# A hybrid layer's kernel: the butterfly folding woven into the first batch's mixer, its low stages multiplied together, and the last division moved to VectorE

## The reference

```python
xl = tanh((x + delta * xp_mu) @ xp_W1.T)          # delta = shifted - x
mur, muw, muk, muv, mug = per-token mixes from xl (rank 32 each)
r, k, v = (x + delta * mu_) @ W_.T                # w and g through rank 64 and tanh
o = rwkv6_scan(r, k, v, -exp(w), bonus)
x = mixer_norm(o) * g * sigmoid(g) @ o_W.T ...
# feed-forward: gelu(butterfly_up(W_exp(x))) -> butterfly_down -> W_con
for stage in range(10):                           # butterfly, dim 1024
    s = 2 ** stage                                # pairs i with i ^ s
    na  = w[..., 0, 0] * a + w[..., 0, 1] * b
    nb2 = w[..., 1, 0] * a + w[..., 1, 1] * b
```

## Time and profile before

| | us |
|---|---|
| median of 3 runs (1972.53 to 1974.41) | 1973.07 |
| the profiled execution's own time | 1972.45 |
| its span | 1970.7 |
| PE busy | 1836.9 (93%) |
| DVE busy | 1026.0 (52%) |
| ACT busy | 745.6 (38%) |
| POOL busy | 689.3 (35%) |

### The profile page before, as it was taken

The page is one execution under the profiler, slowest core; times in us unless marked ns, Lnnn a source line. Parts: engine busy times, 40 slices in busy tenths (PEclk is TensorE's granted clock), DMA queues, the critical chain, the costliest instruction groups (busy, mean ns, idle before and its releaser), DMA issues.

```text
span 1970.7 us, 30530 instructions
## 1 busy us (share of the span) xinstructions
PE 1836.9 (93%) x11604; PEld 1371.8 (70%) x11604; DVE 1026.0 (52%) x2198; ACT 745.6 (38%) x1566; POOL 689.3 (35%) x864
## 2 busy tenths in 40 slices
PE   2759889999999999999999999999999999999878
PEld 2627754798459864798459864798459864798457
DVE  4846355553656355653656355653656355652531
ACT  4732235422451335422451335422451335422341
POOL 4025232532335232532335232532335232532220
PEclk9979899999999999999999999999999999999799
DMA  6000000000000000000000000000000000000000
GB/s 218 0 0 12 1 11 12 1 1 21 2 12 1 1 23 12 1 1 17 6 12 1 1 22 12 1 1 11 11 12 1 1 22 1 1 1 2 10 1 11
DMA packets 17048, 24.11 MB, mean 12 GB/s; under 512 B 960, under 2 KB 15056, under 8 KB 16912
## 3 DMA queue, kind: packets, MB, share of 16 engines
q1 hardware_dynamic: 14944, 15.68, 2.5%
q0 software_dynamic: 1968, 6.56, 0.9%
HBM read 18.04 MB, written 4.19 MB: 11 GB/s over the span
## 4 chain that ended last, share of the span: by engine, by line
PE 89%; DVE 5%; POOL 2%; issue 2%; DMA 1%; ACT 1%; SPq 0%; DVEq 0%; POOLq 0%; ACTq 0%
PE ring L1396 17%; PE ring L1381 17%; PE ring L1436 9%; PE ring L1359 9%; PE ring L1368 6%; PE ring L1533 5%; PE attn_out L1553 4%; PE ring L1491 3%; PE ring L1513 3%; PE ring L1303 2%; PE ring L1516 2%; PE ring L1351 2%; PE ring L1536 2%; PE ring L1405 2%; PE ring L1467 1%
## 5 line engine op out<-in xcount | busy, mean ns | idle before, releaser
L1188 DVE TENSOR_REDUCE maxes<-ring 128x2 f32<-128x768 f32 (+7 forms) x294 | 198.2, 731 | 91.9 <-PE ring L1516 91.1
L1114 DVE COPY_PREDICATED scores_t<-masks,ring 128x512 f32<-128x512 uint16 x224 | 163.8, 731 | 112.4 <-issue 95.8
L1436 PEld LDWEIGHTS ring<-big 128*128 128x128 f32 x1536 | 178.3, 192 | 6.6 <-issue 4.1
L1436 PE MATMUL ring<-big 128*128 128x128 f32 x1536 | 179.7, 275 | 0.7 <-issue 0.6
L597 POOL TENSOR_TENSOR rstd<-mean_var,eps_and_power 128x2 f32<-128x2 f32 x96 | 19.3, 201 | 449.8 <-DVE mean_var L1040 385.9
L653 POOL TENSOR_TENSOR big<-big,decay_blocks 128x256 f32<-128x256 f32 x192 | 140.3, 745 | 103.5 <-issue 84.4
L1396 PE MATMUL ring<-w_down,big 128*128 128x256 f32 x768 | 172.3, 379 | 0.0
L1396 PEld LDWEIGHTS ring<-w_down,big 128*128 128x128 f32 x768 | 144.3, 190 | 18.7
L625 POOL TENSOR_TENSOR mix<-mix,z_t 128x512 f32<-128x512 f32 x80 | 84.8, 1089 | 132.6 <-DVE mix L1087 132.6
L1533 PE MATMUL ring<-big 32*128 32x512 f32 (+3 forms) x1024 | 124.0, 480 | 3.4 <-issue 1.7
L854 ACT ACTIVATE big<-ring,up_bias 128x256 f32<-128x256 f32 x192 | 80.6, 471 | 99.7 <-PE ring L1381 99.7
(11 more groups left out here) (214 smaller groups left out, 3547.0 us busy)
## 6 DMA issues: line engine op xcount, KB each, us to landing
x_in<-in_x SPq DMA_DIRECT2D x8, 512.0 KB, 4.0
out<-x_plus_bias SPq DMA_DIRECT2D x8, 512.0 KB, 2.9
delta<-in_x SPq DMA_DIRECT2D x7, 512.0 KB, 3.9
w_mlp<-in_wm POOLq DMA_DIRECT2D x2, 1024.0 KB, 13.0
big<-in_w_exp_t SPq DMA_DIRECT2D x1, 1028.0 KB, 29.5
big<-in_w_con SPq DMA_DIRECT2D x1, 1024.0 KB, 19.2
big<-in_masks SPq DMA_DIRECT2D x1, 704.0 KB, 6.4
w_r<-in_wr POOLq DMA_DIRECT2D x1, 512.0 KB, 7.1
```

The lines of the kernel that those rows point to most:

```text
L1114: ins = nc.vector.copy_predicated(scores[:, h, :, :], lmask[:, lv, :].bitcast(U16).unsqueeze(1) .to_broadcast([P, NT, P]), chunks)
L1188: nc.vector.tensor_reduce(maxes[:, t % 2, qt, 32 * gs[0] + row:32 * gs[-1] + row + 1:32], banks[:, first:last, lo:hi], AX_X, ALU.max).then ...
L1436: ins = mm(ps[:, tok], kg[:, h, tok], q[:, h, tok], start=True, stop=True)
```

## The change

1. **Low stages first.** For a group of four tiles of one butterfly, the seven stage matrices are multiplied with each other: `mat` makes a stage's four matrices (diagonals on ACT, permuted part on DVE), `prod` multiplies them into the product (PE) and copies it out (ACT, 128x512), and `fin` multiplies the weight by the product. Four groups: two of the down butterfly, two of the up butterfly. `hd` and `hu` are the high stages, now with the scaling on POOL.
2. **Woven.** These steps, with the transposes `tw` into `wup` and the biases, become entries of PROGRAM. `woven` spreads them evenly over the first batch's mixer. The scratch tiles move to places that the mixer leaves free: the MLP's weights, `x`, `z` and `xb`.
3. **Loads by need.** Each load has a semaphore of its own use; x comes third on SP. 17 loads are on POOL, behind three small memsets. The MLP's weights (2 MB) are loaded by SP once the folding is done. The masks come as 16-bit values, without a cast.
4. **The last division** of a batch (t = 3) and the sum after it run on DVE.
5. **Split fill steps.** `k`, `v` and `ga` are halves now; `("v", 1, 0)` and half of `k 1` come ahead of a turn, and `("ga", 1)` comes behind the last `V`.

```diff
+                    [("k", 0, 0), ("k", 0, 1), ("k", 1, 0)], [("k", 1, 1)]],
+                1: [[("k", 2, 0), ("k", 2, 1)], mixed["C"], [], [("k", 3, 0), ("k", 3, 1)], mixed["D"]],
+                2: [[("v", 0, 0), ("v", 0, 1)], [], [], [("v", 1, 0)], [("v", 1, 1)]],
+                3: [[], [], [("ga", 0)], [], [("ga", 1)]]}[t]
...
+def butterfly_steps():
+    def chain(g):
+        o = [("mat", g, 0), ("mat", g, 1)]
+        for k in range(1, LOW):
+            o += [("prod", g, k)] + ([("mat", g, k + 1)] if k + 1 < LOW else [])
+        return o
+    def high(kind):
+        return [(kind, i, t) for i in range(STAGES - LOW) for t in range(NF)]
+    o = chain(0) + high("hd") + [("fin", 0)] + chain(1) + [("fin", 1)]
+    o += chain(2) + [("fin", 2)] + chain(3) + [("fin", 3)] + high("hu") + [("upb",)] + [("tw", n) for n in range(4)]
+    return [(0, *s) for s in o] + [(0, "biases")]
+def woven(main, extra):
+    lead, tail = 4, 14
+    n = len(main) - lead - tail
+    o = main[0:lead]
+    for i in range(n):
+        o += extra[i * len(extra) // n:(i + 1) * len(extra) // n] + [main[lead + i]]
+    return o + main[lead + n:]
...
+                if b == 0:
+                    sp.wait_ge(wup_ready.h, 4)
+                    sp.wait_ge(upb_ready.h, 1)
+                    sp.dma_start(wm1, chunked(dflt["wm1"])).then_inc(mlp_w_in.h, 16)
+                    sp.dma_start(wm2, chunked(dflt["wm2"])).then_inc(mlp_w_in.h, 16)
...
+            def high_scaled(kind, i, t):                                  # POOL
...
+                if n >= NTMP:
+                    pool.wait_ge(high_ready.h, n - NTMP + 1)
+                nc.gpsimd.tensor_scalar(tmp_h[:, n % NTMP, 0:width], src[:, t, 0:width],
+                                        twiddles[:, 0, which, t, st:st + 1], None, ALU.mult).then_inc(*one(tmp_ready))
...
+            def diagonals(g, k):                                          # ACT
...
+                if n >= 2:
+                    act.wait_ge(mat_ready.h, n - 1)
+                for j in range(NCHAIN):
+                    t = NCHAIN * (g % 2) + j
+                    ins = nc.scalar.activation(diag[:, n % 2, j, :], ident[:, :], ACT.Copy,
+                                               scale=twiddles[:, 0, which, t, st:st + 1])
+                ins.then_inc(*one(diag_ready))
+            def product_copied(g, k):
+                act.wait_ge(*bank_full(("prod", g, k)))
+                nc.scalar.activation(product[:, k % 2, :, :].rearrange("p j n -> p (j n)"), bank(("prod", g, k)),
+                                     ACT.Copy).then_inc(*one(prod_ready))
...
+                if t == NG - 1:                                           # DVE, in inverted(t)
+                    dve.wait_ge(*after(inv_spread, NG))
+                    nc.vector.tensor_tensor(osum[t], osum[t], inverse, ALU.mult).then_inc(*one(divided))
+                    dve.wait_ge(*after(divided, NG))
+                    nc.vector.tensor_tensor(osum[t - 1], osum[t - 1], osum[t], ALU.add).then_inc(*one(attn_ready))
...
+            def matrices(g, k):                                           # DVE
...
+                dve.wait_ge(diag_ready.h, n + 1)
...
+                for j in range(NCHAIN):
+                    t = NCHAIN * (g % 2) + j
+                    ins = nc.vector.scalar_tensor_tensor(out=dst[:, j, :], in0=perm[:, st, :],
+                                                         scalar=twiddles[:, mate, which, t, st:st + 1],
+                                                         in1=diag[:, n % 2, j, :], op0=ALU.mult, op1=ALU.add)
+                ins.then_inc(*one(mat_ready))
...
+            def chain_product(g, k):                                      # PE
+                pe.wait_ge(mat_ready.h, step_number(g, k) + 1)
+                if k >= 2:
+                    pe.wait_ge(prod_ready.h, (LOW - 1) * g + k - 1)
+                ps = take(("prod", g, k))
+                for j in range(NCHAIN):
+                    ins = mm(ps[:, j * P:(j + 1) * P], stage_mat[:, k % 2, j, :], product[:, (k - 1) % 2, j, :],
+                             start=True, stop=True)
+                ins.then_inc(*filled(("prod", g, k)))
```

More of the change, by code:

```diff
@@ L181, in psum_keys @@
         return [(b, kind, *at, g) for g in range(HG)]
+    if kind == "prod" or kind == "tw":
+        return [step]
+    if kind == "fin":
+        return [(b, kind, at[0], j) for j in (range(2) if at[0] < 2 else range(4))]
     return []
@@ L551, in hybrid_kernel, with loaded @@
+        def loaded(s):
+            return s.h, 16 * sum(load[2] is s for load in sync_loads + pool_loads)
         x_dram = dflt["x"].rearrange("b (t p) d -> b p t d", p=P)
@@ L689, in _ @@
                     norm(*at)
+                elif kind in ("hd", "hu"):
+                    high_scaled(kind, *at)
+                elif kind == "biases":
+                    pool.wait_ge(*loaded(attn_w_in))
+                    nc.gpsimd.tensor_tensor(bias_f[:, :], bias_f[:, :], down_b[:, :], ALU.add).then_inc(*one(bias_f_ready))
                 elif kind == "mix":
@@ L887, in _ @@
                     turned(*at)
+                elif kind == "mat":
+                    diagonals(*at)
+                elif kind == "prod":
+                    product_copied(*at)
+                elif kind == "fin" and at[0] >= 2:
+                    low_stages_up(*at)
+                elif kind == "tw":
+                    w_up_copied(*at)
                 elif kind == "xl":
@@ L1021, in _ @@
[L1021 to L1023 removed]
+            dve.wait_ge(*loaded(cols_in))
             def after(s, k):
@@ new lines, in low_stages_down, with up_biases @@
+            def low_stages_down(g):
+                for j in range(2):
+                    dve.wait_ge(*bank_full(("fin", g, j)))
+                    t = NCHAIN * (g % 2) + 2 * j
+                    nc.vector.tensor_copy(wdn[:, t:t + 2, :].rearrange("p a n -> p (a n)"),
+                                          bank(("fin", g, j))).then_inc(*one(fin_ready))
+            def up_biases():
+                dve.wait_ge(high_ready.h, 2 * N_HIGH)
+                for m in range(NF):
+                    ins = nc.vector.tensor_tensor(upb[:, m:m + 1], w_raw[:, m, D:UW], col("up_b", m), ALU.add)
+                ins.then_inc(*one(upb_ready))
@@ L1220, in _ @@
+            for b, kind, *at in PROGRAM:
+                if kind == "mat":
+                    matrices(*at)
+                elif kind in ("hd", "hu"):
+                    high_stage_done(kind, *at)
+                elif kind == "fin" and at[0] < 2:
+                    low_stages_down(*at)
+                elif kind == "upb":
+                    up_biases()
+                elif kind == "biases":
+                    attention_bias()
+                elif kind == "mix0":
                     first_mix()
@@ new lines, in low_stages @@
+            def low_stages(g):
+                pe.wait_ge(prod_ready.h, (LOW - 1) * (g + 1))
+                if g < 2:
+                    pe.wait_ge(high_ready.h, N_HIGH)
+                elif g == 2:
+                    pe.wait_ge(*loaded(up_in))
+                for j in range(NCHAIN):
+                    t = NCHAIN * (g % 2) + j
+                    lhs = product[:, (LOW - 1) % 2, j, :]
+                    if g < 2:
+                        ps = take(("fin", g, j // 2)) if j % 2 == 0 else bank(("fin", g, j // 2))
+                        ins = mm(ps[:, j % 2 * D:(j % 2 + 1) * D], lhs, w_mid[:, t, 0:D], start=True, stop=True)
+                        if j % 2:
+                            ins.then_inc(*filled(("fin", g, j // 2)))
+                    else:
+                        mm(take(("fin", g, j))[:, 0:UW], lhs, w_raw[:, t, :], start=True,
+                           stop=True).then_inc(*filled(("fin", g, j)))
@@ new lines, in w_up_turned, with value_bias @@
+            def w_up_turned(n):
+                if n == 0:
+                    pe.wait_ge(high_ready.h, 2 * N_HIGH)
+                ps = take(("tw", n))
+                c, q = n % NC, n // NC
+                for m in range(T // P):
+                    ins = nc.tensor.transpose(ps[:, m * P:(m + 1) * P], w_raw[:, q * (T // P) + m, c * P:(c + 1) * P],
+                                              ident[:, :])
+                ins.then_inc(*filled(("tw", n)))
+            def value_bias():
+                pe.wait_ge(*loaded(attn_w_in))
+                pe.wait_ge(value_rows.h, 1)
+                for c in range(NG // 2):
+                    ins = mm(obank[0][:, 0:D], bias_rows[:, c, :], wo_b[:, c, :], start=(c == 0),
+                             stop=(c == NG // 2 - 1))
+                ins.then_inc(*one(bias_mm))
```

466 lines of the change are left out of this document (210 added, 256 removed).

## The result

The changed kernel takes 2009.97 us (median of 4 runs, 2008.12 to 2012.27) where the kernel before takes 1973.74 (4 runs beside it): a ratio of 1.0185 with a 95% interval of 1.0167 to 1.0202. The forecast was 1986, with a range to 2006. The side was right, but the loss is 36 us and not 13, and the time lies outside the range.

The account below looks back on a forecast made before the run. From 221.4 us on PE bounds the kernel, so only its idle time can be won; the first mixer has room for weaving. 1972.45 + 39 (later Z) - 25 (gains behind it) = 1986 us; range 1956 to 2006, forecast's own 1977 to 1998.

Parts of the forecast that it names:

- Z: Time at which the first batch reaches transpose zt F 0, behind the woven stretch: 221.4 us before, 260 forecast.
- signs that it named for being wrong: Products closer than 4 us, hd taking 15, or steady batches gaining more than 4 us each.
- POOL's scaling: In hd and hu: 0.37 to 0.40 us each, bounded by the 128x256 cast, 0.40, and by L585, 0.91.
- The walk: Step-by-step sum of the woven stretch to Z: 246.5 at full PE clock, clock +11, POOL against DVE +3, so 260.
- the rival that had it: POOL's scaling costs 0.91: hd +13, hu +16, total 2015 us; chance 0.10.
- The gains behind Z: Shorter waits and wo from the division and split steps: 25 us, between 15 and 28.
- the shift of the bank ring: The folding takes 40 ring keys, changing the number of row-max instructions by two: counted as nothing.
- The steps of the chains: 24 folding steps in which nothing overlaps the next: 4.3 us each, 5.2 where the granted clock is 0.5.
- PE becomes the bound: Rival for the woven stretch: all delays are filled, Z = 140, total 1866 us; chance 0.06.
- The high stages do overlap: Rival: POOL and DVE side by side, hd 15, hu 31, products at full clock, Z = 233.5, 1959 us; chance 0.15.
- Neither clock nor ports cost much: Rival for the woven stretch: Z = 246.5 to 249, total 1972 to 1976 us, no change; chance 0.13.
- The loads hide: All loads but the MLP's 2 MB issued by 13 us; those wanted over 100 us behind Z.

Follow-up runs that it names:

- e6: e4 with the second k product whole again, behind the last P.V product of group 0: 1952.12 us, ratio 0.9886.
- e10: Changed kernel with three 128x512 products that nobody reads behind each chain product: 2038.1 us, ratio 1.0334.
- e2: Changed kernel with the matrices of stage k+1 built ahead of the product of stage k: 1960.78 us, ratio 0.9936.
- e9: Changed kernel with the folding not woven: all its steps but the value bias ahead of the first batch's norm: 2037.39 us, ratio 1.0332.
- e1: Changed kernel with the 48 scalings of the high stages on ACT instead of POOL: 1999.67 us, ratio 1.0133.
- e7: Changed kernel with e1's and e2's edits, plus unread products behind chain products and hd steps, two ahead of each chain: 1974.97 us, ratio 1.0006.
- e4: Kernel before with only the last division and sum on DVE and k, v, ga in halves: 1953.29 us, ratio 0.9892.
- e12: Changed kernel with POOL's 48 scalings written as a product of two tensors, the factor's column broadcast: 2004.41 us, ratio 1.0157.

## Why the prediction was wrong, step by step

The forecast was right on the form of the loss: products far apart, ACT's copy directly ahead of its diagonals, ACT idle for most of the stretch, and a gain behind Z that doesn't make up for it. None of the signs that it named for being wrong came. The working went 26 us wrong (2012.27 against 1986), 22 of them in two terms; either of them right would have put the time into the range.

**POOL's scaling, +13.** The step that failed is the price of 0.37 to 0.40, "since L585 is a first call of two elements". The runs don't bear that reason out: the same operation, again POOL's first of its form, takes 0.26 in the changed kernel, so it told nothing of a 128x256 one in either direction. The nearest row was then taken to be a cast of the same size, which has no scalar, and its 0.40 didn't carry over to this form: the scaling takes 0.90 to 0.94, and 1.08 to 1.13 for 257 columns beside DVE's level steps. `hd` took 28.8 instead of 22.3 and `hu` 48.0 instead of 41.5. (The walk has 22.6 for `hd` but adds 22.3.) A second step failed with it and hid half of it: the walk adds POOL's and DVE's time of each high step, 0.78, but in the trace they overlap, and `hd` goes by POOL's 0.90 alone. The upper bound of the sum was exactly the price; the rival that had it got a chance of 0.10 and 2015 us. Its total is near by luck: it too adds the two engines' times, 13 and 16 us more, where 6.5 and 6.5 were measured, and the 9.4 us of gains that stayed away behind Z and 3 more of the walk, which it didn't have, stand in for most of the rest.

**The gains behind Z, 15.6 and not 25.** Each gain that was named came: 17.8 of waits in front of `wo` (22.5 us in eight batches became 4.7) against 15.9, 3.8 of `wo` itself (36.1 us became 32.3) against 4.5, 4.1 in front of the last turn against 4.2. That is 25.7. What was missing is what they cost: 4.2 of the wait for the `k` copy, and 6.0 of PE's busy time elsewhere (in all it is 1694.29 against 1692.09, though `wo` gave 3.8), of which 1.8 are in the score products and 1.5 in `v`. 25.7 - 10.2 = 15.5. e6 shows that the wait comes with the half of `k`. The forecast took the halves as free, and the shift of the bank ring as nothing from the number of row maxima alone; it did not ask what the moved halves stand in front of. It had 15 as its lower bound, for another reason.

**The steps of the chains: right.** 4.3 us at full clock were forecast and 5.2 at half; measured 4.18 (e10) and 5.10. The release of PE took 0.06 and not 0.25. The walk without the scalings is 17 us above its full-clock sum, where 14 were set for the clock and POOL's share in groups 2 and 3; at 0.92 for each of 16 products at half clock up to 14.7 of them are the clock (an estimate). Groups 2 and 3 have 11.6 of the 17 (46.7 us instead of 40.1, 26.9 instead of 21.9); their five products at half clock and three that are so in part are some 6 of them by the same price, and the other 6 were not traced to a cause.

**The mechanism: shown.** e2 changes nothing but the order of two entries and gives 49 us back. Z comes 51.8 earlier by it, nearly all of the 55.0 that it was late. 24 steps times 5.10 less 2.78 would be 56; some are filled by the mixer.

**The rivals.** That PE becomes the bound is refuted (e9: PE busy 67.5 of 179.5). The high stages do overlap, as that rival had it, but at 0.90 a scaling and not 0.40 this makes nothing faster. "Neither clock nor ports cost much" is refuted by e10's 0.92 a step and by e1's 0.48 against 0.84. The loads hide, as forecast: among the 60 longest entries of the waits view of the changed kernel none is for a transfer; the one in its first 40 us is DVE's 6.5 for x, and `delta` starts at 21.04, about where the walk had it.

**The two rules of the Trainium skill.** DVE's high steps take 0.48 with the scalings on ACT and 0.69 to 0.84 with them on POOL. The Trainium skill ("GPSIMD Engine Reference", Key points) names this contention, and the trace agrees that the two slow each other; that one shuts the other out it doesn't show. On the clock, 16 of 24 products ran at the lower level in the changed kernel, 7 in e2 and none in e7; where the mixer's matmuls stand between them (fourth group of e2) they take 1.06 to 1.16 in spite of waits of up to 2.98 us. The Trainium skill ("TensorE: Matmul & The Clock Gate", HAM oscillation) says that bursts with waits between them keep PE at half rate; the trace agrees for the chains that have nothing between their products, and not for every burst behind a wait: the fourth chain's first product, with 3.87 us of wait before it, takes 2.08 in the changed kernel and 1.16 in e1.

## What to carry to other kernels

A list that sets the order on every in-order engine should put an operation that waits for nothing ahead of the copy that waits for PE: here that order alone was worth 49 us, more than the whole idea of weaving (24) and more than moving work between engines (10). Before four side-by-side chains are replaced with one that does less work, count how many of its hand-overs are still covered by something. And when work is set into an idle place of a well-filled stretch, ask what it now stands in front of, as well as which wait it fills. And test the parts of a change by themselves: here the two small edits behind Z gain 20 us alone (e4), and the large one lost 55 ahead of it.

## What the runs showed of the hardware that was not expected

- On POOL a 128x256 tensor times a scalar for each partition takes 0.90 to 0.94 us, the same written as a product of two inputs, with the scalar's column broadcast, 0.60 (e12; both with DVE idle: 0.92 against 0.60), a cast of the same size 0.396. Here the form with two inputs is the cheaper one of the two.
- The same instruction on DVE (128x257, one product and one sum) takes 0.475 with the scalings on ACT (e1) and 0.838 with them on POOL. POOL's own, of 128x257, takes 0.91 in e9 (eight in 7.27, with DVE's high steps at 0.69 beside it) and 1.08 to 1.13 in the changed kernel, where DVE has the level steps beside it too. So each slows the other, but they don't take turns: in `hd` a scaling and a high step, 0.90 and 0.69, go by every 0.90 us.
- From 90.4 to 115 us of the changed kernel, where the chain's products come up to 5.10 us apart, the granted clock is 0.53, near the lower of TensorE's two levels (1.2 GHz), and a product takes 2.08 us where it takes 1.16 at the upper one. With idle products in the gaps (e10) they take 1.16 and the step is 0.92 shorter, but the kernel is 28 us slower.
